# Jumping back instead of spelling out: a rolled loop in three edge passes, and a shorter rest between scattered writes

## The reference

```python
# L0_ffn: attention over 32768 edges of its own, whose scores route the nodes to 4 experts
e = leaky_relu(a_src[src] + a_dst[dst]);  e_max = segment_max(e, dst)
# L1_gnn: typed attention over 50000 edges
attn_score = sum(q_att[etype, col_idx] * k[row_idx], axis=-1);  m = segment_max(score, col_idx)
# L3_gnn: weighted sum over the same edges, taken from their other end
msg = edge_weight[:, None] * h[edge_col];  z = segment_sum(msg, edge_row)
```

## Time and profile before

| what | value |
|---|---|
| median of 3 runs | 6321.1 us (6319.48 to 6324.7) |
| the profiled execution's own time | 6324.7 us |
| its span in the profile | 6323.0 us |
| PE busy / DVE busy / ACT busy / POOL busy | 72% / 54% / 26% / 38% |
| `gat_s`, 72 rounds | 1287 to 1795 us |
| `hgt_s`, 104 rounds | 2434 to 3194 us |
| `wsum_a`, 104 rounds | 5404 to 6027 us |

### The profile page before, as it was taken

The page is one execution under the profiler, slowest core; times in us unless marked ns, Lnnn a source line. Parts: engine busy times, 40 slices in busy tenths (PEclk is TensorE's granted clock), DMA queues, the critical chain, the costliest instruction groups (busy, mean ns, idle before and its releaser), DMA issues. The chain is left out here.

```text
span 6323.0 us, 80166 instructions
## 1 busy us (share of the span) xinstructions
PE 4578.4 (72%) x22972; PEld 3239.2 (51%) x23008; DVE 3396.5 (54%) x7272; ACT 1648.1 (26%) x3833; POOL 2376.8 (38%) x2718
## 2 busy tenths in 40 slices
PE   5867978857757694555659889999999494354458
PEld 2213444635546452444436677768887352344446
DVE  8988962645575454777758644441112234454444
ACT  0955642411212251110100233333222122000022
POOL 0841027455515344555500048821111301577710
PEclk8998999868868896676759989999999697676779
DMA  0003456422221287777737310004333421233310
GB/s 30 2 10 121 188 188 208 122 48 41 41 73 53 56 329 271 239 242 235 243 118 243 98 30 11 11 30 137 102 99 93 108 100 32 90 91 91 90 23 20
DMA packets 406423, 688.65 MB, mean 109 GB/s; under 512 B 116747, under 2 KB 294546, under 8 KB 401450
## 3 DMA queue, kind: packets, MB, share of 16 engines
q1 hardware_dynamic: 309570, 433.42, 21.6%
q0 software_dynamic: 96320, 250.79, 13.3%
q10 hardware_dynamic: 192, 0.15, 0.0%
HBM read 447.15 MB, written 236.36 MB: 108 GB/s over the span
## 5 line engine op out<-in xcount | busy, mean ns | idle before, releaser
L1109 PE MATMUL wsum_a_ps<-wsum_a_hot,wsum_a_rows 128*128 128x128 f32 x1664 | 298.6, 356 | 329.3 <-DVE big L1136 188.7
L1095 POOL DMA_INDIRECT wsum_a_rows<-table,edge_src x416 | 433.6, 1042 | 261.5 <-issue 119.1
L2224 POOL DMA_INDIRECT big<-hgt_table,edge_key x416 | 393.1, 945 | 364.1 <-DVE hgt_s_tmp L2317 219.7
L1109 PEld LDWEIGHTS wsum_a_ps<-wsum_a_hot,wsum_a_rows 128*128 128x128 f32 x1664 | 280.2, 264 | 347.7 <-issue 213.9
L3657 PE MATMUL sagel_ps<-sagel_piece,sagel_high 128*128 128x448 f32 x1050 | 399.5, 380 | 0.8 <-issue 0.8
L3657 PE MATMUL sagel_ps<-sagel_piece,sagel_low 128*128 128x448 f32 x1050 | 385.9, 367 | 0.0
L2307 DVE TENSOR_REDUCE hgt_highest<-hgt_s_pm 128x8 f32<-128x1024 f32 x208 | 253.1, 1218 | 187.7 <-remote 169.1
L2274 PE MATMUL hgt_s_pq<-big 128*128 x1248 | 251.1, 373 | 139.9 <-DVE hgt_s_tmp L2317 76.0
L2224 POOL DMA_INDIRECT big<-gat_table,own_src x288 | 271.8, 944 | 213.1 <-issue 84.0
L2264 PE MATMUL hgt_s_pm<-hgt_s_turned,pick 112*128 112x128 bf16 x1664 | 185.0, 279 | 214.0 <-DVE hgt_highest L2307 179.6
L790 PE MATMUL cnt_ps<-cnt_hot_s,cnt_hot_d 128*128 128x512 bf16 (+1 forms) x1724 | 310.5, 334 | 39.5 <-DVE cnt_hot_s L772 36.1
(11 more groups left out here) (994 smaller groups left out, 11032.9 us busy)
## 6 DMA issues: line engine op xcount, KB each, us to landing
hgt_edge_values<-big SPq DMA_DIRECT2D x104, 512.0 KB
big<-hgt_edge_values SPq DMA_DIRECT2D x104, 512.0 KB, 4.6
x<-counts SPq DMA_DIRECT2D x75, 448.0 KB, 3.3
x<-counts SPq DMA_DIRECT2D x75, 336.0 KB, 2.9
counts<-big SPq DMA_DIRECT2D x25, 832.0 KB, 3.4
counts<-big SPq DMA_DIRECT2D x25, 768.0 KB, 3.3
big<-counts SPq DMA_DIRECT2D x30, 640.0 KB
counts_turned<-big SPq DMA_DIRECT2D x30, 640.0 KB
```

The source lines that it names most:

```text
L1095: nc.gpsimd.indirect_dma_start(rows[n % DEEP][:, u, :], None, table, bass.IndirectOffsetOnAxis(ap=e.src[:, g:g + 1], axis=0)).then_inc(gat ...
L1109: mm = nc.tensor.matmul(ps[r.slot % 2][u][:, k * P:(k + 1) * P], rows[r.slot][:, u, k * P:(k + 1) * P], hot[r.slot % 2][:, u, :], start=Tr ...
L2224: nc.gpsimd.indirect_dma_start(rows[n % DEEP][:, u, :], None, at.table, bass.IndirectOffsetOnAxis(ap=at.index[:, g:g + 1], axis=0)).then_i ...
```

## The change

`rolling` gets a real loop: the middle bodies are executed by a jump back, with `j` in a register of each engine. Everything computed from `r.n`, `r.turn` or `r.j` in these bodies is now computed in registers while the kernel runs. Head and tail stay written out. The strip of the last 279 writes has half the columns.

```diff
@@ def rolling(eng, step, rounds, body=DEEP):
     for c in range(-2, 3):
         step(Round(0, c, rounds, False, body))
-    for j in range((rounds - 8) // body):
+    with eng.Fori(0, (rounds - 8) // body) as j:
         for k in range(body):
             step(Round(j, 3 + k, rounds, True, body, 3))
@@ def program(nc, A, out):
-                pace_too = {"back": c.enter_context(nc.sbuf_tensor("back_pace_too", [P, PACE], F32))[:]}
+                pace_too = {"back": c.enter_context(nc.sbuf_tensor("back_pace_too", [P, PACE // 2], F32))[:]}
```

## The result

The changed kernel takes 6673.9 us (median of 4 runs, 6660.7 to 6677.3) against 6322.9 us for the kernel before on the same chip (6319.5 to 6326.3): a ratio of 1.0553, 95% interval 1.054 to 1.0566. It is 351 us slower; 6374 us was forecast, in a range to 6490.

The account below looks back on a forecast made before the run. In the score stages POOL's gathers and the way back to them were taken to set the pace, in L1_ffn's stage PE. Jumps 8 us plus register work 41 us on 6324.7 us gave 6374 us, range 6290 to 6490.

Parts of the forecast that it names:

- The shorter strip: Beside L1_ffn's networks: 160-column clears save POOL 40 us, its writes end near 4109 us, nobody waits; taken as 0.
- The sum for the loop: Stages driven by `rolling`: 8 us for jumping back plus 41 us for register work, 49 us together.
- Rival 4: L1_ffn's stage: shorter rest makes PE's reports late once in 8 writes, 77 us more, 6451 us; chance 0.05.
- Jumps: Loops in `rolling`: 56 branches back at 291 ns each on DVE, half covered, 8 us (0 to 16).
- Rival 3: `hgt_s` and `gat_s`: each jump back waits 4.43 us for code, 142 us, perhaps half covered; 6445 to 6516; chance 0.12.
- Register work at a restart: Between DVE's release and POOL's restart: 0.4 us at 112 restarts, 92% in the loop, 41 us (10 to 93).
- the gaps called issue: POOL's short idle gaps before gathers in `hgt_s`, 144.2 us in 366, expected to stay unchanged.
- near 49 and each 0.2 to 0.9 us longer: Expected sign in `hgt_s`: POOL's long gaps before L2224 keep their number but lengthen; stage 10 to 40 us longer.
- PE in `gat_s`: Matmuls with experts' columns from registers: register work hidden behind PE's waits, taken as 0; 45 us kept for the range.
- Rival 1: `rolling`'s stages: "remote" waits come from streamed code and the loop ends them, -151 us, 6223 us; chance 0.20.
- Rival 2: POOL's gathers and longer operations cover all the loop's added work: 6325 to 6337 us; chance 0.13.

Follow-up runs that it names:

- the base: Kernel before, with 930 wait values from a load of node numbers masked in two stages the change doesn't touch: ratio 1.0019, 13 us.
- the kernels without the stalls: Clear of 320 columns behind each `edge_scores` gather: with the loop 0.988 to the kernel before; without it, plus 160 columns in `aggregate_t`, 0.9808.
- the three pairs: Loop against no loop in the changed kernel, with the loop alone, and with clears behind `edge_scores` gathers: `gat_s` +19, +24 and +23 us.

## Why the prediction was wrong

Its sign was right, but 305 of the 351 us that made it so come from a term that it put at nothing; the loop alone would have given the sign as well. It failed by one step, **"The shorter strip"**: "Nobody waits for that ... I take 0." The arithmetic of the step came true: a clear of 160 columns took 245 ns (234 forecast), and the writes ended at 4142.4 + 0.98 us, 394 us after their start in place of 434, the 40 us saved. What failed was the view that the strip is only POOL's own time. PE's reports pass in it, and 0.41 us let through a fifth of them. That term alone is 305 us, more than the 300 by which 6374 was missed; the three looped stages are 30 us longer together, and were forecast at 49. The sum for the loop came near; its parts did not, as shown below.

**Rival 4** had the right mechanism, at 0.05. Its price was wrong, 77 us for 305, and so was what I set against it, "a rest stays between any two writes". It took the harm as a part of a stall every eighth write, from the gathers' cycle; but there POOL itself comes to wait for PE's work and stops, and the stall ends 1.72 us behind its last gather, while the writes wait for nobody. 279 of them in a row keep PE at a fifth of its rate for all of their time. The rows had the warning: PE's reports late behind gathers 0.30 us apart, and PE busy 521 of 543 us beside writes with a clear of 378 ns between them. The change put the rest between the two.

The other steps, from the changed kernel:

- *Jumps.* A branch took 56 ns on DVE and 208 on PE, as assumed; 0.16 us for addition, branch and register work on DVE where I had 0.29.

```profile
L696 PEldq COMPARE_BRANCH  x56: 76/208/249, 1381.9 to 6333.2; - x56
L696 DVEq ALU_OP  x56: 40/40/40, 1382.1 to 6341.2; - x56
L696 DVEq COMPARE_BRANCH  x56: 50/56/69, 1382.2 to 6341.3; - x56
L696 DVEq FUSED_REGOPS  x56: 62/63/80, 1305.1 to 6318.1; - x56
```

- *Rival 3* is out: the longest of PE's 56 branches took 249 ns. Behind each of the seven jumps back in `gat_s` PE's next idle time is 0.23 to 1.41 us, 5.4 us together, none near 4.43. Code came in that stage in 11 packets with 0.13 MB, on queues q8 and q14, in place of 36 with 0.46 MB when it was written out. The rule of the Trainium skill (page "Runtime: NRT & Kernel Launch", section "Instruction fetch mechanics"), by which these jumps would have stalled, does not show in this trace; the same section gives PE room for 2048 instructions, which would hold the body, and the trace fits that figure and not the window of two pages that the prediction took.
- *Register work at a restart*, 41 us (the 92% in it is 96 of 104 rounds; "88 of 104" was a slip). A cycle of `hgt_s`, as in the earlier trace rows:

```profile
2811.48 0.94 POOL L2224 DMA_INDIRECT big<-hgt_table,edge_key  x1 [5.02 <-DVE hgt_s_tmp L2317]
...
2820.91 0.95 POOL L2224 DMA_INDIRECT big<-hgt_table,edge_key  x1 [0.30 <-issue]
2823.12 1.23 DVE L2307 TENSOR_REDUCE hgt_highest<-hgt_s_pm 128x1024 f32 x1 [3.96 <-remote]
...
2824.97 1.22 DVE L2317 TENSOR_TENSOR hgt_s_tmp<-big,hgt_s_pq 128x1024 f32<-128x1024 f32 x1
...
2826.46 0.94 POOL L2224 DMA_INDIRECT big<-hgt_table,edge_key  x1 [4.61 <-DVE hgt_s_tmp L2317]
```

  It takes 14.98 us where it had taken 14.66, and from DVE's release to POOL's restart 3.34 us against 3.17: 0.17 us more and not 0.4, in the one cycle that was read of each kernel. Over the stage (POOL before L2224, us and times):

```profile
  DVE hgt_s_tmp L2317: 222.7, 55
  issue: 155.3, 361
```

  55 pauses of 4.05 us in place of 49 of 4.48 are only 3.0 us more; the gaps called issue, forecast as unchanged, grew by 11.1 us. With the loop alone, in another session, it is the pauses, 60 with 243.7 us against 49 with 211.3 in the base, and issue grew by 3.5. That the pauses would stay "near 49 and each 0.2 to 0.9 us longer" was wrong both times: more of them, not longer ones.
- *PE in `gat_s`*, taken as 0 with 45 us kept for the range. DVE's L2307 there waited 52.1 us for PE and 90.3 for late reports before, and now:

```profile
  PE gat_s_pm L2264: 90.9, 33
  remote: 78.7, 18
```

  Together 27 us more, for a stage 19 us longer. But in the kernels without the stalls the two rise by 4 us only, where the loop still costs 23, so these waits are not what the three pairs share. What they share is a term that the prediction does not have:
- *Table loads on ACT in `gat_s`.* ACT's functions need a table in place, and a load of one is an instruction of ACT, `ACT_TABLE_LOAD`. Written out, the stage had one, in front of L2455, the Gelu of the experts. With the loop each of the 8 bodies has two, one in front of the copy L2235 and one in front of L2455:

```profile
L2235 ACT ACT_TABLE_LOAD x8 | 10.3, 1283 | 2.2 <-issue 2.1
L2455 ACT ACT_TABLE_LOAD x8 | 10.3, 1283 | 0.1
```

  That is 15 more, 19.2 us of ACT, in all three kernels with the loop. The one in front of L2235 stands on the way to POOL's restart:

```profile
1384.49 1.28 ACT L2235 ACT_TABLE_LOAD   x1 [0.35 <-issue]
...
1385.78 0.25 ACT L2235 COPY big<-big 128x64 f32 x1
...
1386.78 0.94 POOL L2224 DMA_INDIRECT big<-gat_table,own_src  x1 [4.02 <-ACT big L2235]
```

  POOL's waits for L2235 rose from 77.4 us in 24 to 100.6 in 26, and without the stalls from 9.3 in 7 to 42.6 in 25. The stage's three costs, 19, 24 and 23 us, are near these loads; no run takes them away alone, so that they are the cause is argued and not shown.
- *Rival 1* is out: remote waits stay where code comes in 2 to 4 packets on q8 in place of 14 to 31, and ACT's in `hgt_s` even rise, from 38.7 us in 10 to 138.6 in 47. These answer to the earlier trace rows and, for `hgt_s`, to the earlier trace rows:

```profile
DVE wsum_a_hot L1125 <- remote: 199.9, 26, 14.5
DVE hgt_highest L2307 <- remote: 162.8, 40, 5.1
ACT gat_s_turned L2249 <- remote: 100.3, 19, 22.0
```

```profile
q8 instruction: 3, 0.05, 0.0%
```

- *Rival 2*, all covered, is out: the loop alone costs 61 us over the base, against a forecast of 49.

What stays open: by what path a POOL that issues indirect DMAs holds up PE's reports and not DVE's, whether the rest alone decides or the time from write to write has a part, why the knee is where it is, and why it lies higher, or is blurred, in the score stages. Shown is that the shorter strip costs some 300 us, all in that stage, that POOL's clears alone cost nothing, that fewer rows a write bring nothing back, and that the place of the tiles is not it; the DMA engines are busy 2 to 6% with and without the loss.

## What to carry to other kernels

A pause that looks like waste can be what another engine lives on: before cutting one, find the place in the same trace where the pause is already shorter and look at every engine there, also those that wait for nothing of the one that pauses. Where PE's results are taken late in bursts while POOL issues indirect DMAs less than about 0.5 us apart, try a clear of some 320 columns behind each: it slowed the gathers by a fifth and made this kernel 2% faster. When code that was written out becomes a loop, count each engine's instructions again, and not only the jumps: here ACT got 15 table loads of 1.28 us that no line of the kernel asks for.

## What the hardware did that I had not expected

PE's reports came 8.34 and 7.74 us apart, while DVE's came in 0.34 us and DMA engines were busy 5%. The rest between POOL's indirect DMAs has a knee between 0.48 and 0.51 us beside L1_ffn's networks: 522.6 us for the networks above it and 659.7 just below. 64 rows in a write in place of 128 took 897 ns in place of 978 and were as harmful (833.4 against 817.7 us). Clears that kept POOL busy 69 of 76 us did nothing to PE. The loop brought ACT two table loads of 1.28 us a body.
